# One order of q for scores and relative term, and the rows' scalings moved from VectorE to ScalarE

## The chip, the core and the metric

The kernel runs on one core of a Trainium2 chip. The core has TensorE (PE in the profile, its weight loads PEld), VectorE (DVE), ScalarE (ACT), GpSimd (POOL) and SyncE (SP), which here does nothing but issue DMA transfers and wait. Each engine works through its own instructions in the order in which the program has them. Engines wait for each other by semaphores. The metric is the device time of the whole kernel in microseconds.

## The reference

Four batches of 1024 tokens with 128 features go through attention with 16 heads of 8 features, causal, with a relative term, and then through a feed-forward net. Cut to what matters here:

```python
q, k, v = split_heads(x @ Wq + bq), split_heads(x @ Wk + bk), split_heads(x @ Wv + bv)   # x is normalised per row
scores = jnp.einsum('bhid,bhjd->bhij', q, k)
rel = jnp.einsum('bhid,pd->bhip', q, rel_key)                # P = 256 rows of rel_key
rel_idx = jnp.clip(j - i + p - 1, 0, p - 1)
bias = jnp.take_along_axis(rel, rel_idx, axis=3)
logits = jnp.where(causal, (scores + bias) * scale, -inf)
attn = softmax(logits); out = attn @ v; y = out @ Wo + bo
x = x + layernorm(y)
x = x + layernorm(ffn(layernorm(x)))                         # 128 -> 512 -> 512 -> 512 -> 128
```

## The kernel before, in words

There are three stages, all of them written out in program order by hand. The change is in stage one and in what stage two reads.

Stage one (`sync_one`, `gpsimd_one`, `vector_one`, `scalar_one`, `tensor_one`) goes over the batches b = 0 to 3, and each round of it works on two batches at once. For batch b+1 VectorE makes the statistics of the rows (L482 to L489), ScalarE the root (`std`, L630), VectorE the reciprocal and the offset (`rstd`, `nmr`) and the eight scalings of 128x128 (`xh`, L501). TensorE transposes `xh` into the PSUM tile `p_tr` (L731), ScalarE copies that to `xT` (L637), and TensorE projects it to q and k (L741) and to v (L749). For batch b ScalarE takes q and k out of PSUM (`qf` L664, `kf` L666); VectorE reduces k to extremes (`k_ext`), makes `k_sel` and `own`; TensorE computes from them a bound on the scores, again in `p_tr` (`bound`, L759 to L761). The bound's maximum goes to `gap_max` (L508), the bound itself as two bf16 parts to `m_parts` (ScalarE L699, VectorE L513). The next transposes write into the same `p_tr`, so they wait for both (`transposes` waits `s_mneg`, `s_gap` and `s_mr`).

q and k are written as three bf16 parts each (`q_parts`, `k_parts`: a part 0 by ScalarE, the remainder by VectorE, part 1 by ScalarE, part 2 by VectorE) and stored to DRAM (`q_dram`, `k_dram`) part by part by SP, since stage two needs each of them on other partitions. Stage two also needs q in a second order. Its scores (L1089) take blocks of 128 neighbouring rows i, its relative term (L1023) takes for one r of 128 the rows r, 128 + r, 256 + r and so on, eight a head. The kernel before stores q twice: `q_dram` in the order of the rows, and `qr_dram` with the eight rows of one r side by side. The second comes from `turn_query` (L650), which has ScalarE copy each of the three parts into `q_turned`. The remainder of batch b+1's parts can only start when the stores of batch b's parts have landed (L681, L682).

SP's order in batch 1 matters: it stores batch 0's bound, waits until all stores of batch 0 have landed, issues the loads of stage two's first unit (`q_rows` L413, `k_sb` L334, `q_sb` L323), and then the stores of batch 1.

Stage one ends with the first fill of stage two's table `even_b`: TensorE makes eight chunks (`relative`), six copied by ScalarE (L1036) and two by VectorE (L619, L620). ScalarE then does the three `turn_query` of batch 3 and, at L716, waits for `s_low`, which VectorE raises after its two chunks (`low_k`, L532). Stage two takes units of 8 heads: scores and relative chunks on TensorE, additions on VectorE, exponentials on ScalarE, products with v on TensorE. Stage three is the feed-forward net.

## Time and profile before

| | us |
|---|---|
| median of 3 runs | 739.33 |
| lowest and highest | 736.46, 739.54 |
| the profiled execution | 737.71 |
| its span, first to last instruction | 735.6 |
| TensorE busy | 645.0 |
| ScalarE busy | 572.5 |
| VectorE busy | 538.9 |
| DMA moved | 52.82 MB |

2.1 us of the profiled execution lie outside its span. The median of the runs is 1.6 us above the profiled execution. Stage one takes the first 103 to 107 us, stage two runs until about 480 to 490 us, stage three to the end. A busy share is an average over the three and says little on any one of them; what follows is read by stage.

### The profile page before, as it was taken

To read this page: it belongs to the slowest core of one execution; us is meant where nothing else is said; L and a number is where in the kernel's file an instruction comes from. 1 tells how busy PE (TensorE), PEld (TensorE's weight loads), DVE (VectorE), ACT (ScalarE), POOL (GpSimd) and SP (SyncE) were. 2 spreads that over 40 slices of the span, in tenths; PEclk is the share of its full clock that TensorE was granted. 3 is DMA by queue.
4 is the path that set the end of the run, shared out by engine and by line. 5 is a ranking of instruction groups with operands and counts; after the bars stand their busy time and mean duration, and the time that the engine had idled before them with its cause. 6 is when DMAs were issued, how large, how long until landed. Compare 5 with 4: busy or idle time off the path is not lost.

```text
span 735.6 us, 18944 instructions
## 1 busy us (share of the span) xinstructions
PE 645.0 (88%) x8066; PEld 467.9 (64%) x8066; DVE 538.9 (73%) x923; ACT 572.5 (78%) x660; POOL 246.6 (34%) x175
## 2 busy tenths in 40 slices
PE   4877669999999999999999999978799898998993
PEld 2333336676766766867667667655588687786682
DVE  5885787787687877786877777765677568588546
ACT  2794977988989889889898898786577868677573
POOL 2100270360640912705408128010271441731801
PEclk9988767999999999999999999997999999999997
DMA  7487423152241231521412314040300000000001
GB/s 229 113 228 219 134 84 90 38 129 66 51 111 40 71 96 35 130 69 43 106 52 68 100 34 123 27 158 1 101 1 1 0 1 1 1 29 0 6 24 59
DMA packets 39175, 52.82 MB, mean 72 GB/s; under 512 B 5656, under 2 KB 29640, under 8 KB 36680
## 3 DMA queue, kind: packets, MB, share of 16 engines
q1 hardware_dynamic: 39088, 51.58, 25.6%
q8 instruction: 65, 1.06, 0.6%
q14 instruction: 22, 0.18, 0.1%
HBM read 39.00 MB, written 11.81 MB: 69 GB/s over the span
## 4 chain that ended last, share of the span: by engine, by line
PE 53%; DVE 13%; ACT 12%; issue 5%; POOL 2%; DVEq 0%; ACTq 0%; POOLq 0%
PE p_o L1114 16%; PE p_s L1089 13%; PE p_z L1788 8%; PE p_z L1791 8%; DVE probs L1215 6%; ACT probs L1332 6%; PE p_s L1023 5%; POOL hid_lo L1709 1%; DVE res L1969 1%; ACT hid_hi L1892 1%; ACT o_acc L1341 1%; ACT even_b L1036 1%; ACT odd_b L1036 1%; PE p_o L1126 1%; DVE hid_lo L1993 1%
## 5 line engine op out<-in xcount | busy, mean ns | idle before, releaser
L1089 PE MATMUL p_s<-q_sb,k_sb 96*128 96x128 bf16 (+1 forms) x1600 | 172.2, 250 | 9.2 <-ACT probs L1332 3.5
L1332 ACT ACTIVATE probs<-p_s 128x1024 f32<-128x1024 f32 x160 | 156.6, 1017 | 18.5 <-DVE p_s L1224 10.8
L1114 PE MATMUL p_o<-probs,v_sb 128*32 128x128 f32 (+1 forms) x3200 | 159.7, 331 | 7.5 <-ACT o_acc L1341 4.7
L992 POOL TENSOR_SCALAR_AFFINE_SELECT even_b<-even_b 128x2048 f32<-128x2048 f32 x31 | 75.9, 2449 | 259.6 <-ACT even_b L1036 259.6
L1332 ACT ACTIVATE probs<-probs 128x1024 f32<-128x1024 f32 x128 | 133.5, 1055 | 36.1 <-DVE probs L1215 35.8
L1089 PEld LDWEIGHTS p_s<-q_sb,k_sb 96*128 96x128 bf16 x1600 | 113.9, 100 | 68.5 <-issue 30.3
L1215 DVE TENSOR_TENSOR probs<-p_s,even_b 128x1024 f32<-128x1024 f32 x96 | 114.9, 1218 | 16.8 <-PE p_s L1089 16.8
L1114 PEld LDWEIGHTS p_o<-probs,v_sb 128*32 128x32 f32 x3200 | 84.6, 111 | 40.9 <-issue 13.9
L1788 PE MATMUL p_z<-hid_hi,h_hi 128*128 128x512 f32 x256 | 102.1, 399 | 1.7 <-POOL hid_lo L1709 1.7
L1023 PE MATMUL p_s<-q_rows,rel_w 72*128 72x64 bf16 x2048 | 83.8, 196 | 19.6 <-DVE probs L1215 8.7
L1791 PE MATMUL p_z<-hid_lo,h_hi 128*128 128x512 f32 x256 | 100.9, 394 | 0.0
L1023 PEld LDWEIGHTS p_s<-q_rows,rel_w 72*128 72x128 bf16 x2048 | 75.4, 100 | 30.9 <-DVE probs L1215 11.0
L1993 DVE TENSOR_TENSOR hid_lo<-act_f,hid_hi 128x512 fp32r<-128x512 f32 x64 | 55.6, 881 | 41.5 <-ACT hid_hi L1892 41.4
L996 POOL TENSOR_SCALAR_AFFINE_SELECT even_b<-even_b 128x2048 f32<-128x2048 f32 x31 | 73.8, 2380 | 7.0 <-POOL even_b L992 7.0
L1891 ACT ACTIVATE act_f<-p_z,sh_c 128x512 f32<-128x512 f32 x64 | 44.3, 692 | 28.6 <-PE p_z L1791 28.5
L1236 DVE COPY even_b<-p_s 128x1024 f32<-128x1024 f32 x35 | 42.7, 1220 | 21.3 <-PE p_s L1023 21.0
L1788 PEld LDWEIGHTS p_z<-hid_hi,h_hi 128*128 128x128 f32 x256 | 48.2, 188 | 13.5 <-POOL hid_lo L1709 2.6
L1791 PEld LDWEIGHTS p_z<-hid_lo,h_hi 128*128 128x128 f32 x256 | 48.3, 189 | 10.7
L1236 DVE COPY odd_b<-p_s 128x896 f32<-128x896 f32 x32 | 34.7, 1086 | 23.6 <-PE p_s L1023 22.4
L1215 DVE TENSOR_TENSOR probs<-p_s,odd_b 128x1024 f32<-128x1024 f32 x32 | 39.1, 1222 | 15.0 <-PE p_s L1089 15.0
L1892 ACT ACTIVATE hid_hi<-p_z,sh_c 128x512 fp32r<-128x512 f32 x64 | 44.1, 689 | 0.0
L1709 POOL TENSOR_TENSOR hid_lo<-act_f,hid_hi 128x512 fp32r<-128x512 f32 x32 | 42.4, 1326 | 2.6
(182 smaller groups left out, 846.2 us busy)
## 6 DMA issues: line engine op xcount, KB each, us to landing
k_sb<-k_dram SPq DMA_DIRECT2D x48, 192.0 KB
q_sb<-q_dram SPq DMA_DIRECT2D x16, 576.0 KB
q_rows<-qr_dram SPq DMA_DIRECT2D x42, 192.0 KB
q_dram<-q_parts SPq DMA_DIRECT2D x12, 256.0 KB, 3.0
k_dram<-k_parts SPq DMA_DIRECT2D x12, 256.0 KB, 3.2
qr_dram<-q_turned SPq DMA_DIRECT2D x12, 256.0 KB, 3.4
x_all<-in_L_attn_x_dram SPq DMA_DIRECT2D x4, 512.0 KB, 4.4
every<-in_L_ffn_h_w_dram SPq DMA_DIRECT2D x2, 1024.0 KB, 8.3
```

Of the source, the lines that this page charges most:

```text
L992: nc.gpsimd.affine_select(out=far, in_=near, compare_op=ALU.is_ge, fill=0.0, base=-1 - r, pattern=[[0, QB], [-1, MCH * RCH]], channel_mult ...
L996: nc.gpsimd.affine_select(out=near, in_=near, compare_op=ALU.is_ge, fill=MASKED, base=r, pattern=[[0, QB], [1, MCH * RCH]], channel_multip ...
L1023: last = nc.tensor.matmul(slot[:, x * QB:(x + 1) * QB], rel_w[0:ROWS, w0:w0 + BLK], q[:, r, :, :], start=True, stop=True)
L1089: last = nc.tensor.matmul(slot[:, c:c + n * BLK], k_sb[hg][:, h * S + j * BLK:h * S + (j + 1) * BLK], ap(q_sb[hg], at, [[HG * S, KROWS], [ ...
L1114: last = nc.tensor.matmul(p_o[32 * h:32 * h + 32, at:at + blocks * BLK], v_sb[hg][:, j, h * 32:(h + 1) * 32], probs[n % PBUFS][:, h, col * ...
L1215: last = nc.vector.tensor_tensor(probs[m % PBUFS][:, hp * 2:hp * 2 + 2, :], columns(slot, 0, run), term, ALU.add)
L1236: nc.vector.tensor_copy(to, got).then_inc(t_cd, 1)
L1332: nc.scalar.activation(to, got, ACT.Exp, scale=SCALE).then_inc(t_exp, 1)
L1788: nc.tensor.matmul(to[:, :], whi[w][:, j, cols], hi[j], start=(j == 0), stop=False)
L1791: last = nc.tensor.matmul(to[:, :], whi[w][:, j, cols], lo[j], start=False, stop=(j == len(hi) - 1))
L1892: nc.scalar.activation(hid_hi[k][l % 2][:, o, :], bank(tile)[:, :], ACT.Gelu, scale=sc).then_inc(f_ghi, 1)
L1993: nc.vector.tensor_tensor(hid_lo[k][l % 2][:, o, :], act_f[k][:, o, :], hid_hi[k][l % 2][:, o, :].bitcast(F32), ALU.subtract).then_inc(f_l ...
```

## The change

q is stored in one order only. The 1024 rows of a head are 8 blocks i of 128, and a row in its block is r = 4·s + l. The order before was (i, s, l) in `q_dram` and (s, l, i) in `qr_dram`; now there is (s, i, l) alone (`mixed`), with LO = 4 values of l side by side. The permutation is made by the operations that were there already, in their access patterns: ScalarE's part 0, VectorE's remainder of q, and both parts of the bound. `turn_query`, `q_turned`, `qr_dram` and their waits are gone. The score matmul reads q in runs of four, the relative matmul reads every fourth element. The sign of the bound is no longer turned; the row of k that meets it is -1 in place of 1.

The scalings `xh` of batches 1 to 3 are made by ScalarE (`scaled`), the statistics of batch b+2 stand at the end of VectorE's round b, and ScalarE's check of the weights' low bits (`low_bits`) stands after the parts. `largest_scores`, a branch for inputs with a wide bound that is not taken here, is fitted to the new order.

```diff
-        for copy in range(PARTS):
-            sp.dma_start(to, ap(qr_dram, u * (UH * S) + half * width,
+            sp.dma_start(to, ap(q_dram, u * (UH * S) + half * width,
...
+    def natural(tile):
+        return tile.rearrange("p (i r l) -> p r i l", i=NB, l=LO)
+    def mixed(tile):
+        return tile.rearrange("p (r i l) -> p r i l", i=NB, l=LO)
...
         def batch(b, first, last):
             if b == 1:
-                for done in (s_qst, s_kst, s_rst):
+                for done in (s_qst, s_kst):
                     sp.wait_ge(done, 16 * PARTS)
-                sp.dma_start(q_rows[:, :], ap(qr_dram, 0, [[DROW, PARTS * HD], [0, PARTS], [1, UH * S]])).then_inc(t_qr[0], 16)
+                sp.dma_start(q_rows[:, :], ap(q_dram, 0, [[DROW, PARTS * HD], [0, PARTS], [1, UH * S]])).then_inc(t_qr[0], 16)
...
-                if not last:
-                    turned(b, part)
...
         def layernorm(b, first):
             dve.wait_ge(s_std, b + 1)
+            if not first:
+                dve.wait_ge(s_xh, b)
             nc.vector.reciprocal(rstd[:, :], std[:, :]).then_inc(s_ln, 1)
...
+            if not first:
+                return
             dve.wait_ge(s_ln, b * LNS + 5)
-            if not first:
-                dve.wait_ge(s_tr, b * 2)
             for t in range(NB):
                 last = nc.vector.tensor_scalar(xh[:, t, :], tile(t), rstd[:, t:t + 1], nmr[:, t:t + 1],
                                                ALU.mult, ALU.add)
...
         def shift_rest(b):
-            nc.vector.scalar_tensor_tensor(out=m_parts[:, 1, :], in0=p_tr[0:H, :], scalar=-1.0, in1=m_parts[:, 0, :],
-                                           op0=ALU.mult, op1=ALU.subtract).then_inc(s_mr, 1)
+            nc.vector.tensor_tensor(mixed(m_parts[:, 1, :]), natural(p_tr[0:H, :]), mixed(m_parts[:, 0, :]),
+                                    ALU.subtract).then_inc(s_mr, 1)
...
         def batch(b, first, last_batch):
-            if not last_batch:
-                layernorm(b + 1, False, None if first else lambda: gap(b - 1))
-            else:
+            if not first:
                 gap(b - 1)
-            if not first:
                 shift_rest(b - 1)
...
-            nc.vector.tensor_tensor(q_rest[:, :], qf[:, :], q_parts[:, 0, :], ALU.subtract).then_inc(s_rest, 1)
+            nc.vector.tensor_tensor(mixed(q_rest[:, :]), natural(qf[:, :]), mixed(q_parts[:, 0, :]), ALU.subtract).then_inc(s_rest, 1)
...
+            if b + 2 < B:
+                layernorm(b + 2, False)
...
+        def scaled(b):
+            act.wait_ge(s_xin, b * 16 + 16)
+            act.wait_ge(s_ln, b * LNS + 5)
+            act.wait_ge(s_tr, b * 2)
+            for t in range(NB):
+                last = nc.scalar.activation(xh[:, t, :], x_all[:, b * S + t * E:b * S + (t + 1) * E], ACT.Identity,
+                                            scale=rstd[:, t:t + 1], bias=nmr[:, t:t + 1])
+            last.then_inc(s_xh, 1)
...
-        def turn_query(b, part):
-            nc.scalar.activation(turned_view(q_turned, part), untouched_view(q_parts, part),
-                                 ACT.Identity).then_inc(s_turned, 1)
...
-            nc.scalar.activation(q_parts[:, 0, :], qf[:, :], ACT.Identity).then_inc(s_hi, 1)
+            nc.scalar.activation(mixed(q_parts[:, 0, :]), natural(qf[:, :]), ACT.Identity).then_inc(s_hi, 1)
...
-                nc.scalar.activation(m_parts[:, 0, j * 512:(j + 1) * 512], p_tr[0:H, j * 512:(j + 1) * 512],
-                                     ACT.Identity, scale=-1.0).then_inc(s_mneg, 1)
-            if not last_batch:
-                turn_query(b, 2)
+                nc.scalar.activation(mixed_half(m_parts[:, 0, :], j),
+                                     p_tr[0:H, j * 512:(j + 1) * 512].rearrange("p (i r l) -> p i r l", i=NB // 2, l=LO),
+                                     ACT.Identity).then_inc(s_mneg, 1)
+            if b + 2 < B:
+                scaled(b + 2)
...
-                turn_query(b, 0)
-                turn_query(b, 1)
-                turn_query(b, 2)
...
-        q = q_rows[:, :].rearrange("k (h r i) -> k r h i", h=UH, i=NB)
+        q = q_rows[:, :].rearrange("k (h r i l) -> k r l h i", h=UH, i=NB, l=LO)
-            last = nc.tensor.matmul(slot[:, x * QB:(x + 1) * QB], rel_w[0:ROWS, w0:w0 + BLK], q[:, r, :, :],
+            last = nc.tensor.matmul(slot[:, x * QB:(x + 1) * QB], rel_w[0:ROWS, w0:w0 + BLK], q[:, r // LO, r % LO],
...
-                    at = h * S + i * BLK
+                    at = h * S + i * LO
-                                            ap(q_sb[hg], at, [[HG * S, KROWS], [2 * BLK, n], [1, BLK]]),
+                                            ap(q_sb[hg], at, [[HG * S, KROWS], [2 * LO, n], [NB * LO, BLK // LO], [1, LO]]),
```

Line numbers in the rows of after are those of the changed file, some ten to fifteen lower. ScalarE's queue before, from the bound of batch 1 (`m_parts`) through batch 2:

```order
L699 ACTIVATE m_parts<-p_tr 16x512 x2
L654 ACTIVATE q_turned<-q_parts 128x1024
L630 ACTIVATE std<-var_e 128x8
L664 ACTIVATE qf<-p_q,bq_c 128x1024
L666 ACTIVATE kf<-p_k,kb_c 128x1024
L637 ACTIVATE xT<-p_tr 128x512 x2
L674 ACTIVATE q_pos<-qf 128x1024
L683 ACTIVATE q_parts<-qf 128x1024
L685 ACTIVATE k_parts<-kf 128x1024
L654 ACTIVATE q_turned<-q_parts 128x1024
L689 ACTIVATE q_parts<-q_rest 128x1024
```

And the same stretch after:

```order
L689 ACTIVATE m_parts<-p_tr 16x4x32x4
L622 ACTIVATE std<-var_e 128x8
L689 ACTIVATE m_parts<-p_tr 16x4x32x4
L637 ACTIVATE xh<-x_all,nmr,rstd 128x128 x8
L656 ACTIVATE qf<-p_q,bq_c 128x1024
L658 ACTIVATE kf<-p_k,kb_c 128x1024
L629 ACTIVATE xT<-p_tr 128x512 x2
L665 ACTIVATE q_pos<-qf 128x1024
L673 ACTIVATE q_parts<-qf 128x1024
L675 ACTIVATE k_parts<-kf 128x1024
L677 ACTIVATE q_parts<-q_rest 128x1024
```

The eight scalings stand where the third `q_turned` of the batch stood; the other two leave no replacement. On VectorE the stretch from the parts of k in batch 0 to the extremes of k in batch 1 reads, before:

```order
L532 TENSOR_TENSOR k_parts<-k_rest,k_parts 128x1024
L482 BN_STATS stats<-x_all 128x6 x8
L486 BN_AGGR mv<-stats 128x2 x8
L489 TENSOR_SCALAR var_e<-mv 128x8
L508 TENSOR_REDUCE gap_max<-p_tr 16x1
L493 RECIPROCAL rstd<-std 128x8
L495 SCALAR_TENSOR_TENSOR nmr<-mv,rstd 128x8
L501 TENSOR_SCALAR xh<-x_all,rstd,nmr 128x128 x8
L513 SCALAR_TENSOR_TENSOR m_parts<-p_tr,m_parts 16x1024
L543 TENSOR_REDUCE k_ext<-kf 128x1
```

and after:

```order
L524 TENSOR_TENSOR k_parts<-k_rest,k_parts 128x1024
L474 BN_STATS stats<-x_all 128x6 x8
L478 BN_AGGR mv<-stats 128x2 x8
L481 TENSOR_SCALAR var_e<-mv 128x8
L485 RECIPROCAL rstd<-std 128x8
L487 SCALAR_TENSOR_TENSOR nmr<-mv,rstd 128x8
L500 TENSOR_REDUCE gap_max<-p_tr 16x1
L505 TENSOR_TENSOR m_parts<-p_tr,m_parts 16x1024
L532 TENSOR_REDUCE k_ext<-kf 128x1
```

The eight `xh` are gone, and the reciprocal stands ahead of `gap_max`. SP's queue after, from the stores of batch 0 to the loads of the first unit (before, a store `qr_dram<-q_turned` stood behind each pair, nine stores a batch in place of six):

```order
L397 DMA q_dram<-q_parts 16x8x1024
L397 DMA k_dram<-k_parts 16x8x1024
L397 DMA q_dram<-q_parts 16x8x1024
L397 DMA k_dram<-k_parts 16x8x1024
L397 DMA q_dram<-q_parts 16x8x1024
L397 DMA k_dram<-k_parts 16x8x1024
L394 DMA m_dram<-m_parts 16x2x1024
L410 DMA q_rows<-q_dram 72x1x8192
```

Nothing else moved on SP there: the loads still wait for the stores of batch 0.

## Rows read from the trace of the kernel before

**Rows 1.** The page: the span.
```profile
span 735.6 us, 18944 instructions
```

**Rows 2.** Busy time in 130 to 480 us (PE, PEld, DVE, ACT, POOL, clock, DMA).
```profile
130.00:480.00 350.00, 330.03 (x6127) 243.43 (x6124) 272.53 (x277) 304.02 (x318) 137.29 (x71) 0.99 0.28 73
```

**Rows 3.** Groups by line and shape, ScalarE, 0 to 110 us (busy, mean ns, idle before).
```profile
L654 ACT ACTIVATE q_turned<-q_parts 128x1024 bf16<-128x1024 bf16 x12 | 23.5, 1978 | 0.0
...
L637 ACT ACTIVATE xT<-p_tr 128x512 f32<-128x512 f32 x8 | 4.7, 596 | 8.9 <-PE p_tr L731 8.9
...
L685 ACT ACTIVATE k_parts<-kf 128x1024 bf16<-128x1024 f32 x4 | 4.2, 1047 | 0.0
...
L630 ACT ACTIVATE std<-var_e 128x8 f32<-128x8 f32 x4 | 0.8, 197 | 5.7 <-DVE var_e L489 5.7
```

**Rows 4.** Timeline, batch 1 and turn to 2 (start, duration, engine, [idle before <-releaser]).
```profile
45.16 0.60 ACT L637 ACTIVATE xT<-p_tr 128x512 f32<-128x512 f32 x1 [0.20 <-PE p_tr L731]
...
57.00 0.59 ACT L699 ACTIVATE m_parts<-p_tr 16x512 bf16<-16x512 f32 x1 [1.93 <-PE p_tr L761]
...
57.50 1.94 ACT L654 ACTIVATE q_turned<-q_parts 128x1024 bf16<-128x1024 bf16 x1
...
59.44 1.09 ACT L664 ACTIVATE qf<-p_q,bq_c 128x1024 f32<-128x1024 f32 x1
...
60.01 2.13 DVE L501 TENSOR_SCALAR xh<-x_all,rstd,nmr 128x128 f32<-128x128 f32 x8
...
62.17 1.21 DVE L513 SCALAR_TENSOR_TENSOR m_parts<-p_tr,m_parts 16x1024 bf16<-16x1024 f32 x1
...
63.53 1.66 PE L731 MATMUL p_tr<-ident,xh 128*128 128x128 f32 x8 [4.58 <-DVE m_parts L513]
64.44 0.60 ACT L637 ACTIVATE xT<-p_tr 128x512 f32<-128x512 f32 x1 [2.91 <-PE p_tr L731]
```

**Rows 5.** Timeline, ScalarE and VectorE, batch 2 and the turn to batch 3.
```profile
72.02 1.06 ACT L683 ACTIVATE q_parts<-qf 128x1024 bf16<-128x1024 f32 x1 [5.25 <-DMA k_dram<-k_parts]
...
73.11 1.23 DVE L566 TENSOR_TENSOR q_rest<-qf,q_parts 128x1024 f32<-128x1024 f32 x1 [5.44 <-ACT q_parts L683]
...
80.81 1.21 DVE L513 SCALAR_TENSOR_TENSOR m_parts<-p_tr,m_parts 16x1024 bf16<-16x1024 f32 x1
...
84.51 1.22 DVE L543 TENSOR_REDUCE k_ext<-kf 128x1 f32<-128x1024 f32 x1 [2.49 <-ACT kf L666]
```

**Rows 6.** Timeline, SP's queue: first and last store of batch 0, loads, batch 1.
```profile
34.56 0.63 SPq L396 DMA_DIRECT2D q_dram<-q_parts  x1
...
40.42 0.74 SPq L396 DMA_DIRECT2D qr_dram<-q_turned  x1
...
44.19 0.84 SPq L413 DMA_DIRECT2D q_rows<-qr_dram  x1
...
56.24 2.62 SPq L396 DMA_DIRECT2D k_dram<-k_parts  x1
```

**Rows 7.** DMA issues from 34.3, 38.2 and 56.2 us (last: us to landing).
```profile
q_dram<-q_parts SPq DMA_DIRECT2D x1, 256.0 KB, 3.0
...
qr_dram<-q_turned SPq DMA_DIRECT2D x2, 256.0 KB, 3.8
...
k_dram<-k_parts SPq DMA_DIRECT2D x1, 256.0 KB, 15.7
```

**Rows 8.** Timeline, VectorE and ScalarE, end of stage one.
```profile
97.15 1.22 DVE L508 TENSOR_REDUCE gap_max<-p_tr 16x1 f32<-16x1024 f32 x1 [1.71 <-PE p_tr L761]
...
101.08 5.80 ACT L654 ACTIVATE q_turned<-q_parts 128x1024 bf16<-128x1024 bf16 x3
...
106.19 1.22 DVE L532 TENSOR_TENSOR k_parts<-k_rest,k_parts 128x1024 bf16<-128x1024 f32 x1
...
107.45 1.94 ACT L1332 ACTIVATE probs<-p_s 128x1024 f32<-128x1024 f32 x2 [0.56 <-DVE k_parts L532]
```

**Rows 9.** The chain that ended last, in stage two (start, duration, what).
```profile
120.04 0.47 PE p_s L1023 x16
```

More of the change, by code:

```diff
@@ L32 @@
 PARTS = 3
+LO = 4
 ROWS = PARTS * PARTS * HD
@@ L253, in build @@
     m_parts = sb("m_parts", [H, MPARTS, S], BF16, one)
-    q_turned = sb("q_turned", [128, PARTS, S], BF16, one)
     pone = ExitStack()
@@ L1471, in head @@
             sp.wait_ge(e_part, g * EPARTS + EPARTS)
-            sp.dma_start(ap(m_dram, g * S, [[BLK, NB], [DROW, MPARTS], [1, BLK]]), parts[:, :, :]).then_inc(e_out, 16)
+            for part in range(MPARTS):
+                sp.dma_start(ap(m_dram, part * DROW + g * S, [[LO, NB], [NB * LO, BLK // LO], [1, LO]]),
+                             parts[:, part, :].rearrange("p (r l) -> p r l", l=LO)).then_inc(e_out, 16)
         with sp.If(taken(sp)):
```

62 lines of the change are left out of this document (23 added, 39 removed).

## The prediction

> **What bounds the kernel now.** I read the stretches first. From 130 to 480 us TensorE is busy 330 of 350 us at a granted clock of 0.99, so stage two is TensorE's, and a change can shorten it only on TensorE [rows 2]. Nothing of the change takes an instruction off TensorE. What can get shorter is stage one, and the chain that ended last is to be followed there by the timeline, queue by queue.
>
> The turn from batch 1 to batch 2 shows how stage one hangs together. The second half of the bound is copied at 57.00 (it waited 1.93 us for TensorE), the third `q_turned` runs from 57.50 for 1.94 us, then `qf` starts at 59.44 and `kf` follows, ending at about 61.5. Meanwhile VectorE scales the rows from 60.01 to 62.14 and only then makes the bound's remainder (`m_parts`, 62.17, 1.21 us). The transposes wait 4.58 us for it and start at 63.53; ScalarE, idle for 2.91 us, copies `xT` from 64.44 [rows 4]. So ScalarE and VectorE hold each other up.
>
> The next place is batch 2. ScalarE cannot write part 0 of q until the stores of batch 1 have landed: it idles 5.25 us until 72.02 on the last `k_dram` store, and VectorE idles 5.44 us behind it [rows 5]. That store was issued at 56.24 and took 15.7 us to land, behind the loads of stage two's first unit, which were issued from 44.19 [rows 6, 7]. From 72.02 VectorE works practically without a gap to the bound's remainder at 80.81, ends it at 82.02, and then waits 2.49 us for ScalarE's `kf`: the extremes of k of batch 3 start at 84.51 [rows 5]. They head the chain of VectorE's work that leads to `own`, to batch 3's bound and with it to the end of stage one.
>
> The last place is that end. ScalarE runs three `q_turned` from 101.08 for 5.80 us, yet the first exponentials, at 107.45, are released by VectorE's `k_parts`, which runs from 106.19 [rows 8].
>
> **The change part by part.** *The twelve `q_turned`.* Each is 1.978 us [rows 3], 23.5 us of ScalarE in all. Nine of them stand in batches 0 to 2. The third of each batch stands ahead of the next `qf`; there the eight scalings take its place. An activation of 8 columns is 0.197 us, one of 512 is 0.596 us [rows 3]; by straight line one of 128 columns is 0.30 us alone, and as two long ones overlap by about 0.1 us (two exponentials take 1.94 us together, [rows 8], where one copy alone is 1.05 us, [rows 3]) a row of eight should take 0.2 us each, 1.6 to 1.9 us. The bounds are 8 x 0.197 = 1.6 and 8 x 0.596 = 4.8 us. I take 1.9, nearest to the line between the rows. So the slot ahead of `qf` stays as it is: 0 us. The last three, 5.8 us, save nothing either, because at 107.45 ScalarE waits for `low_k` (L716), and VectorE's queue there is untouched: 0 us, with 0 to -0.6 as bounds, the 0.56 us of idle time being all that ScalarE's side ever had to do with it [rows 8]. The other `q_turned` of batches 0 to 2 stood beside TensorE's projections and bound and gave ScalarE slack that it now has more of.
>
> *The scalings off VectorE, the remainder of the bound ahead.* 2.13 us go from between `gap_max` and the bound's remainder [rows 4]. After the change `gap_max` (57.0 to 58.2) is followed by the remainder to 59.4, the transposes are done before `kf` ends at 61.5, and `xT` follows `kf` at once: 61.5 in place of 64.44, so 2.9 us a turn. This is gained at two turns, since at the first one (batch 0 to 1) the scalings stay ahead of the transposes on either engine. But the second turn's gain only counts as far as the DMA lets batch 2 go, and so it does not enter the sum; it sets its early bound.
>
> *Six stores a batch in place of nine.* Batch 0's nine stores are issued from 34.56 on; the last, issued at 40.42, lands 3.8 us later at 44.2, and the loads go out at 44.19 [rows 6, 7]. The first landed 3.0 us after its issue [rows 7], at 37.6, so nine took 0.83 us each. Six are through at 37.6 + 5 x 0.83 = 41.7. The loads go out at 41.7 if the bound's remainder of batch 0 has been stored by then, for which SP waits first; without the scalings ahead of it VectorE makes it by about 39.9. That is 2.5 us earlier. Behind the loads the last `k_dram` store had seven stores before it and now has five: 2 x 0.83 = 1.65 us. So it lands at 56.24 + 15.7 - 2.5 - 1.65 = 67.8 in place of 71.94, and ScalarE's part 0 of batch 2 starts at 67.85 in place of 72.02: -4.2 us. Bounds: the loads start no earlier and only the missing stores count, -1.65 us; or the stores land before they are needed.
>
> *The turn from batch 2 to 3.* VectorE started `q_rest` at 73.11 and ended at 82.02, 8.9 us [rows 5], with a gap of 0.3 us for a part that ScalarE made late behind `q_turned`. From 68.95 it ends at 77.6. ScalarE, with no `q_turned` between, copies part 0 of q and k, waits for VectorE, copies parts 1 until about 72.4, copies the bound until 73.4, and ends `kf` at 75.5. VectorE is the later one, so the 2.49 us of idle time are gone and the extremes of batch 3 start at 77.6 in place of 84.51: -6.9 us. The early bound is TensorE's: between `xT` of a batch (45.16) and the copy of its predecessor's bound (57.00) pass 11.8 us from start to start [rows 4]; with the second half of `xT` of batch 3 at about 59.6 the bound's copy starts at 71.4, `qf` at 72, `kf` of batch 3 ends at 74.1, -10.4 us. The late bound, from -1.65 in place of -4.2, is -4.3 us; if nothing at all lands earlier, 71.9 + 9.8 = 81.7, -2.8 us.
>
> *The permutation in ScalarE's and VectorE's own operations.* Part 0 of q, the remainder and the bound now read or write in runs of four elements. The only permuted copy in the trace is `q_turned`, one bf16 element at a time at a stride of 256 bytes, at 1.978 us against 1.047 us for an ordered one [rows 3]. Runs of four f32 lie nearer to the ordered row: 0 us. Were part 0 of q and both bound copies as slow as `q_turned`, 1 to 2 us a batch would come back in three batches, in ScalarE's slack for the most part.
>
> *TensorE's reads.* The relative matmul reads 64 columns, eight bf16 side by side in the row before and now every fourth element; the score matmul reads runs of four with gaps. Sixteen relative matmuls take 0.47 us of the chain, 29 ns each [rows 9]. The new patterns are in no row. Below, nothing can be gained. Above, each read might suffer as ScalarE's did, 1.978 / 1.047 = 1.89 times: 2048 x 29 x 0.89 = 53 us for the relative matmuls alone. I take 0, since the slow row has one element to a place and the new reads have two or four side by side within 16 bytes.
> The Trainium skill ("SBUF — State Buffer", section "Door 1: The DMA port swizzle") has a rule that bears on this: SBUF is read in lines of 16 bytes, and at least two hits in a row on a line are needed for the full rate. `q_turned` has one hit, and the trace agrees with 1.978 us against 1.047. The relative matmul now has two, just enough by the rule, which makes rival A the case in which the rule is too kind to TensorE; no row here shows two hits on TensorE.
>
> **The sum.** 737.7 (span 735.6 and 2.1 outside it, [rows 1]) - 6.9 = 730.8 us. The median of the runs lay 1.6 above the profiled execution; a median is forecast, so I say 731.
>
> **The rivals.** *A, TensorE reads slower.* Place: L1023 and L1089 in stage two, where TensorE has only 20 of 350 us idle [rows 2]. For it: TensorE takes an element from each partition every 0.45 ns (64 columns in 29 ns), over twice as fast as ScalarE (1024 in 1.047 us, [rows 3]), so two neighbours within 16 bytes need not be enough for it. Against it: the slow row has one element to a place, the new pattern two. It ends slower than before from 6.9 / 2048 = 3.4 ns a relative matmul, 12% of 29 ns. At the full factor, relative matmuls alone, 731 + 53 = 784, at a third of it 749.
> *B, the stall stays.* The stores are held by the loads, which are as many bytes as before, and the missing stores save nothing that is waited for; the extremes start at 81.7, -2.8 us: 735. For it: the store before took 15.7 us behind them [rows 7]. Against it: both stores and loads start earlier by SP's own order.
> *C, dear scalings.* Eight at 0.596 us are 4.8, 2.9 more than the slot, in two turns, and 2.6 more in the first. `kf` of batch 3 then ends at about 79.7: -4.8 us, 733. For it: scale and bias come from SBUF per row. Against: the 0.197 us of a small activation with the same engine.
> *D, more gained.* The stores land before batch 2 asks: -10.4 us, 727; in batch 3 TensorE idles less before its bound.
>
> **How the numbers follow.** Forecast with C and D, -4 to -10.4 us: 0.77 (C 0.05, D 0.10). B or a small part of A that eats most of the gain, within 0.5% (3.7 us, about what a measurement of this kernel can tell): 0.10. A, slower: 0.13, of which 0.12 above 743. So faster 0.77, same 0.10, slower 0.13. The likeliest case's own range is 727 to 735, widened by 1.6 at either side for the runs; the 8 in 10 range leaves out A and ends where B does, 725 to 737.
>
> **What would show it.** ScalarE's `q_parts` of batch 2 starting near 68, `xT` of batch 3 right behind `kf`, eight `xh` activations near 0.2 us apart, `k_ext` of batch 3 near 77.6, the first `probs` near 100.5 still released by VectorE's `k_parts`, sixteen L1023 matmuls (a lower line number now) still 0.47 us in stage two and an unchanged length from the first `probs` to the end. It is wrong if relative matmuls last over 32 ns in a row, if `k_dram` still lands at 71, or if the first exponentials gain over a microsecond on VectorE's `k_parts`.

## The result, and the profile after

The changed kernel takes 778.7 us (median of 4 runs, 774.2 to 783.4), the kernel before, run beside it, 738.1 (4 runs). The ratio is 1.055, 95% interval 1.051 to 1.059. The forecast was 731 (725 to 737), faster; it came out slower. The profiled execution took 777.35 us. The first three views of it are the page's span, the stretch 130 to 480 us (columns as in [rows 2]), and TensorE's relative term and its largest group of scores, by line and shape over the whole span; the last line is one step of the chain that ended last and answers to [rows 9].

```profile
span 775.6 us, 18917 instructions
```
```profile
130.00:480.00 350.00, 338.58 (x5486) 260.43 (x5485) 243.88 (x246) 277.41 (x286) 123.27 (x63) 0.99 0.25 65
```
```profile
L1010 PE MATMUL p_s<-q_rows,rel_w 72*128 72x64 bf16 x2048 | 139.4, 235 | 13.1 <-DVE probs L1202 5.2 <-DVE even_b L1223 3.5 <-ACT probs L1319 2.1
L1076 PE MATMUL p_s<-q_sb,k_sb 96*128 96x256 bf16 x704 | 113.1, 278 | 1.9 <-ACT probs L1319 1.2 <-issue 0.3 <-DVE even_b L612 0.3
```
```profile
124.50 0.94 PE p_s L1010 x16
```

L1010 is the old L1023, L1076 the old L1089. Against [rows 2], TensorE is busier (338.6 of 350 us) and gets less done: 5486 matmuls in place of 6127, at the same granted clock of 0.99. Sixteen relative matmuls take 0.94 us in the chain, in place of 0.47: 59 ns each, not 29. Before, the same group had these totals, and the score matmuls of 256 columns were as long as they are now (the kernel before, same view):

```profile
L1023 PE MATMUL p_s<-q_rows,rel_w 72*128 72x64 bf16 x2048 | 83.8, 196 | 19.6 <-DVE probs L1215 8.7 <-ACT kf L666 5.5 <-ACT probs L1332 3.5
L1089 PE MATMUL p_s<-q_sb,k_sb 96*128 96x256 bf16 x704 | 112.8, 279 | 5.6 <-DVE probs L1215 3.0 <-ACT probs L1332 1.3 <-issue 1.2
```

So reading every fourth element costs, reading runs of four doesn't. The busy time of the relative matmuls rose by 55.6 us. In the stretch 130 to 480 us TensorE's idle time fell from 20 to 11.4 us, so a part of the longer reads filled time in which it had waited before.

Stage one gained next to nothing. ScalarE and VectorE in the turn to batch 2, in batches 2 and 3 and at the end, and GpSimd beside them (timelines; the rows answer to [rows 4, 5, 8]):

```profile
56.75 3.18 ACT L637 ACTIVATE xh<-x_all,nmr,rstd 128x128 f32<-128x128 f32 x8
59.84 1.09 ACT L656 ACTIVATE qf<-p_q,bq_c 128x1024 f32<-128x1024 f32 x1
...
61.83 1.06 ACT L629 ACTIVATE xT<-p_tr 128x512 f32<-128x512 f32 x2
...
69.71 1.06 ACT L673 ACTIVATE q_parts<-qf 128x1024 bf16<-128x1024 f32 x1 [5.88 <-DMA k_dram<-k_parts]
...
107.18 1.94 ACT L1319 ACTIVATE probs<-p_s 128x1024 f32<-128x1024 f32 x2 [6.50 <-DVE k_parts L524]
```
```profile
79.25 1.20 DVE L532 TENSOR_REDUCE k_ext<-kf 128x1 f32<-128x1024 f32 x1
...
81.61 1.50 DVE L537 TENSOR_TENSOR k_ext<-k_ext,g_ext 128x2 f32<-128x2 f32 x1
...
83.33 4.72 DVE L545 TENSOR_SCALAR k_sel<-hmask,k_ext 128x64 f32<-128x64 f32 x2
87.96 1.27 DVE L549 SCALAR_TENSOR_TENSOR own<-kf,g_ext,qf 128x1024 f32<-128x1024 f32 x1
...
90.29 2.22 DVE L555 TENSOR_TENSOR q_rest<-qf,q_parts 128x1024 f32<-128x1024 f32 x1
...
96.19 1.22 DVE L500 TENSOR_REDUCE gap_max<-p_tr 16x1 f32<-16x1024 f32 x1 [2.55 <-PE p_tr L749]
...
105.92 1.23 DVE L524 TENSOR_TENSOR k_parts<-k_rest,k_parts 128x1024 bf16<-128x1024 f32 x1
```
```profile
80.75 2.36 POOL L979 TENSOR_SCALAR_AFFINE_SELECT even_b<-even_b 128x2048 f32<-128x2048 f32 x1 [46.13 <-ACT even_b L1023]
83.34 2.36 POOL L983 TENSOR_SCALAR_AFFINE_SELECT even_b<-even_b 128x2048 f32<-128x2048 f32 x1 [0.23 <-POOL even_b L979]
85.65 2.36 POOL L979 TENSOR_SCALAR_AFFINE_SELECT even_b<-even_b 128x2048 f32<-128x2048 f32 x1
88.23 3.22 POOL L983 TENSOR_SCALAR_AFFINE_SELECT even_b<-even_b 128x2048 f32<-128x2048 f32 x1 [0.23 <-POOL even_b L979]
```

The operations of GpSimd are its selects, which make the masks in the table `even_b`. `k_ext` of batch 3 starts at 79.25, 5.3 us earlier than in [rows 5]. But then two small operations of VectorE last as long as GpSimd's selects: the first ends at 83.11, when the select that began at 80.75 ends (80.75 + 2.36), and `k_sel`, 128x64 elements twice, ends at 88.05 with the third select (88.01). In the kernel before, the first select came 7.1 us later, when `k_sel` was done:

```profile
87.27 0.42 DVE L556 TENSOR_SCALAR k_sel<-hmask,k_ext 128x64 f32<-128x64 f32 x2
87.61 1.28 DVE L560 SCALAR_TENSOR_TENSOR own<-kf,g_ext,qf 128x1024 f32<-128x1024 f32 x1
```
```profile
87.85 3.25 POOL L992 TENSOR_SCALAR_AFFINE_SELECT even_b<-even_b 128x2048 f32<-128x2048 f32 x1 [53.39 <-ACT even_b L1036]
```

So `own` starts at 87.96, not earlier than the 87.61 of before, `gap_max` is 1.0 us and the first exponentials are 0.3 us earlier than in [rows 8]. From the first exponentials to the end it is 668.4 us (775.6 - 107.18), before 628.2 (735.6 - 107.45): the loss lies in the part that reads the new order.

Two questions follow: which read costs, and by what rule; and what takes back the gain of stage one.

### The profile page after: what moved, and what is told of

It reads as the page before. It is cut to its first block, busy times and chain, and to the rows that moved or that the text cites. A ratio compares the mean times of both kernels' runs of the same rounds, so it can differ in the third digit from the quotient of the medians.

```text
span 775.6 us, 18917 instructions
## 1 busy us (share of the span) xinstructions
PE 692.6 (89%) x8066; PEld 516.7 (67%) x8066; DVE 536.1 (69%) x899; ACT 565.0 (73%) x672; POOL 245.3 (32%) x175
## 3 DMA queue, kind: packets, MB, share of 16 engines
q8 instruction: 65, 1.06, 0.6%
## 4 chain that ended last, share of the span: by engine, by line
PE 60%; DVE 16%; ACT 6%; issue 3%; POOL 2%; DVEq 0%; POOLq 0%; ACTq 0%
PE p_o L1101 16%; PE p_s L1076 13%; PE p_s L1010 12%; PE p_z L1781 7%; PE p_z L1784 7%; DVE probs L1202 7%; ACT probs L1319 2%; POOL hid_lo L1702 1%; DVE p_s L1207 1%; DVE res L1962 1%; DVE even_b L1223 1%; ACT hid_hi L1885 1%; PE p_o L1113 1%; DVE hid_lo L1986 1%; PE p_pre L1722 1%
## 5 line engine op out<-in xcount | busy, mean ns | idle before, releaser
L1319 ACT ACTIVATE probs<-p_s 128x1024 f32<-128x1024 f32 x160 | 158.9, 1020 | 43.4 <-PE p_s L1076 18.0
L1076 PE MATMUL p_s<-q_sb,k_sb 96*128 96x128 bf16 (+1 forms) x1600 | 169.2, 246 | 3.7 <-ACT probs L1319 1.5
L979 POOL TENSOR_SCALAR_AFFINE_SELECT even_b<-even_b 128x2048 f32<-128x2048 f32 x31 | 73.8, 2381 | 282.3 <-ACT even_b L1023 275.4
L1076 PEld LDWEIGHTS p_s<-q_sb,k_sb 96*128 96x128 bf16 x1600 | 114.2, 99 | 60.6 <-issue 35.0
L1010 PE MATMUL p_s<-q_rows,rel_w 72*128 72x64 bf16 x2048 | 139.4, 235 | 13.1 <-DVE probs L1202 5.2
L1010 PEld LDWEIGHTS p_s<-q_rows,rel_w 72*128 72x128 bf16 x2048 | 125.1, 113 | 23.6 <-DVE probs L1202 7.3
L1101 PEld LDWEIGHTS p_o<-probs,v_sb 128*32 128x32 f32 x3200 | 83.8, 111 | 42.9 <-issue 11.0
L1986 DVE TENSOR_TENSOR hid_lo<-act_f,hid_hi 128x512 fp32r<-128x512 f32 x64 | 54.5, 862 | 42.9 <-ACT hid_hi L1885 42.7
L983 POOL TENSOR_SCALAR_AFFINE_SELECT even_b<-even_b 128x2048 f32<-128x2048 f32 x31 | 73.9, 2385 | 7.0 <-POOL even_b L979 6.7
L1223 DVE COPY even_b<-p_s 128x1024 f32<-128x1024 f32 x35 | 42.8, 1222 | 36.7 <-PE p_s L1010 36.7
L1023 ACT ACTIVATE odd_b<-p_s 128x896 f32<-128x896 f32 x32 | 29.2, 913 | 20.6 <-PE p_s L1010 19.8
```

The lines of the kernel that those rows point to most:

```text
L979: nc.gpsimd.affine_select(out=far, in_=near, compare_op=ALU.is_ge, fill=0.0, base=-1 - r, pattern=[[0, QB], [-1, MCH * RCH]], channel_mult ...
L983: nc.gpsimd.affine_select(out=near, in_=near, compare_op=ALU.is_ge, fill=MASKED, base=r, pattern=[[0, QB], [1, MCH * RCH]], channel_multip ...
L1010: last = nc.tensor.matmul(slot[:, x * QB:(x + 1) * QB], rel_w[0:ROWS, w0:w0 + BLK], q[:, r // LO, r % LO], start=True, stop=True)
L1076: last = nc.tensor.matmul(slot[:, c:c + n * BLK], k_sb[hg][:, h * S + j * BLK:h * S + (j + 1) * BLK], ap(q_sb[hg], at, [[HG * S, KROWS], [ ...
L1101: last = nc.tensor.matmul(p_o[32 * h:32 * h + 32, at:at + blocks * BLK], v_sb[hg][:, j, h * 32:(h + 1) * 32], probs[n % PBUFS][:, h, col * ...
L1223: nc.vector.tensor_copy(to, got).then_inc(t_cd, 1)
```

## The experiments

Each ran on the chip beside the kernel before, whose medians lay between 737.2 and 739.2 us; ratios are against it. The table has the start of the first exponentials (probs) and the span, both of one profiled execution each. That execution can lie off the median: for before_read it is the slowest of 4 (784.3), for two_masks the fastest of 13 (735.2). The starts vary as well: before_read changes nothing before the table's fill in batch 3, yet ScalarE waits 7.02 us for batch 1's last store in place of 5.25. A difference of a microsecond or two between two starts is thus not evidence by itself; the medians and the lengths of operations are.

| kernel | median us | ratio, 95% interval | probs | span |
|---|---|---|---|---|
| before | 738.1 | | 107.45 | 735.6 |
| changed | 778.7 | 1.055 (1.051, 1.059) | 107.18 | 775.6 |
| side: changed, neighbours read | 735.9 | 0.998 (0.996, 1.000) | 106.60 | 733.8 |
| before_read: before, every fourth read | 781.0 | 1.057 (1.054, 1.060) | 109.72 | 782.2 |
| lo2: changed, LO = 2 | 841.2 | 1.140 (1.134, 1.145) | 106.13 | 840.1 |
| lo1: LO = 1 | 1263.0 | 1.712 (1.706, 1.719) | 112.79 | 1260.9 |
| lo8: LO = 8 | 911.9 | 1.233 (1.226, 1.241) | 105.94 | 916.5 |
| side_dve: side, scalings by VectorE | 736.4 | 0.998 (0.996, 1.000) | 107.11 | 732.4 |
| side_masks: side, masks late | 733.7 | 0.994 (0.992, 0.996) | 104.00 | 731.7 |
| two_orders: before, order of stage one | 738.6 | 1.000 (0.998, 1.002) | 108.75 | 736.8 |
| two_masks: two_orders, masks late | 740.5 | 1.003 (1.001, 1.004) | 108.33 | 733.5 |
| before_masks: before, masks late | 740.9 | 1.003 (1.001, 1.005) | 109.82 | 738.4 |
| cheap_turn_masks: changed, cheap ordered copy, masks late | 742.2 | 1.005 (1.003, 1.006) | 111.16 | 740.0 |
| best: that, low_k early | 735.5 | 0.996 (0.994, 0.997) | 106.45 | 734.3 |
| late_lowk_sp: cheap_turn_masks, store moved | 735.3 | 0.995 (0.994, 0.997) | 105.45 | 733.6 |
| best_sp: best, store moved | 735.9 | 0.995 (0.993, 0.997) | 103.84 | 734.2 |

### Which read costs

The first kernel is the changed one with one read put back, so that the relative term takes q values of other rows:

```diff
-        q = q_rows[:, :].rearrange("k (h r i l) -> k r l h i", h=UH, i=NB, l=LO)
+        q = q_rows[:, :].rearrange("k (h r i) -> k r h i", h=UH, i=NB)
...
-            last = nc.tensor.matmul(..., rel_w[0:ROWS, w0:w0 + BLK], q[:, r // LO, r % LO],
+            last = nc.tensor.matmul(..., rel_w[0:ROWS, w0:w0 + BLK], q[:, r, :, :],
```

> The changed kernel with one difference: the relative matmuls (L1010) read eight neighbouring elements of q, as they did before the change, from the rows that are stored in the new order. Their values are so those of other rows of q; everything else is as in the changed kernel. Theory (the read of every fourth element halves TensorE's rate): sixteen relative matmuls fall from 0.93 back to 0.47 us, time about 778.7 - 40 = 738. Rival (the stored order or the scores' runs of four cost the time, through the loads or the score matmuls): it stays within 5 us of 778.

The mirror of it is the kernel before with the other read, again with values of other rows:

```diff
-        q = q_rows[:, :].rearrange("k (h r i) -> k r h i", h=UH, i=NB)
+        q = q_rows[:, :].rearrange("k (h r i l) -> k r l h i", h=UH, i=NB, l=4)
...
-            last = nc.tensor.matmul(..., rel_w[0:ROWS, w0:w0 + BLK], q[:, r, :, :],
+            last = nc.tensor.matmul(..., rel_w[0:ROWS, w0:w0 + BLK], q[:, r // 4, r % 4],
```

> The kernel before, changed in one place: the 2048 relative matmuls read every fourth of 32 neighbouring elements of q_rows (two in each 16 bytes) where they read eight neighbours; they thus take q values that belong to other rows, and nothing else moves. Theory 'lines' (TensorE reads at full rate only with four wanted bf16 in each 16 bytes; two of them cost 58 ns in place of 29 per 64 columns): sixteen relative matmuls take 0.93 us in the chain, 0.195 us more mean by line, and the time is 738 + 41 = 779 us, within 3. Theory 'whole change' (the loss needs the new storage, the scalings or the new order of stage one beside the read): 738 us, and sixteen stay at 0.47 us.

They mirror each other in time, too: 735.9 and 781.0. The relative matmuls by line, of side and of before_read:

```profile
L1010 PE MATMUL p_s<-q_rows,rel_w 72*128 72x64 bf16 x2048 | 82.8, 195 | 15.8 <-DVE probs L1202 8.7 <-ACT probs L1319 3.5 <-DVE even_b L612 1.2
```
```profile
L1023 PE MATMUL p_s<-q_rows,rel_w 72*128 72x64 bf16 x2048 | 139.5, 235 | 18.3 <-ACT kf L666 6.0 <-DVE probs L1215 5.2 <-DVE even_b L1236 3.5
```

This one access pattern is the whole loss, with either form of stage one: 42.8 us from side to changed, 42.9 from before to before_read. What else the change did is worth 1.3 us (side against its own kernel before, 737.2), an interval that just reaches no change. before_read lies 2 us above the 779 of its expectation, within the 3 us given there.

### By what rule

LO is the number of neighbours that the storage keeps together. The scores then read runs of LO, the relative term every LO-th element. The theory of lines says that the 16 bytes of SBUF that hold an element (a line) are what is paid for, and counts the wanted bf16 in each line touched: the scores have LO of them, the relative term 8 / LO. Three kernels change one number (`LO = 4` to 2, 1, 8).

> LO = 2: the relative matmul reads every second element (4 bytes apart), the scores read pairs with gaps. Three theories. (8 bytes) TensorE needs two wanted elements in each 8 bytes: both patterns have them, relative matmuls 29 ns, scores unchanged, about 738. (neighbours) only directly neighbouring elements go at full rate: relative matmuls stay at 58 ns, scores unchanged, about 778. (lines) it is wanted elements per 16 bytes, and four are needed: relative matmuls back to 29 ns, but the scores' pairs now double, 294912 columns at 0.42 ns more, about 738 + 120 = 858.

> LO = 1: the relative matmul reads eight neighbours, the scores read single elements 16 bytes apart. All theories: relative matmuls at 29 ns, scores at half rate; four score matmuls of 256 columns 1.0 in place of 0.54 us, up to 120 us more than 738, so about 850. If the scores have slack, less. If a 16 byte pitch costs more than an 8 byte pitch, over 900.

> LO = 8: the relative matmul reads elements 16 bytes apart, one to each 16 bytes; the scores read runs of eight. (8 bytes) one wanted element in 8 bytes costs the same as at LO = 4: 58 ns, about 778. (lines) one to each 16 bytes instead of two costs double again, 116 ns: about 778 + 100 = 880.

Steps of the chain that ended last, of lo2 (four score matmuls of 256 columns, and the relative term), of the kernel before (the same four), and of lo8 (the relative term), all at a granted clock of 1.00:

```profile
118.52 1.02 PE p_s L1076 x4
119.54 0.47 PE p_s L1010 x16
```
```profile
119.50 0.54 PE p_s L1089 x4
```
```profile
121.90 1.81 PE p_s L1010 x16
```

| wanted bf16 in 16 bytes | ns for 64 columns | from |
|---|---|---|
| 8 | 29 | before, relative, 0.47 / 16 |
| 4 | 29 | lo2, relative, 0.47 / 16 |
| 2 | 59 | changed, relative, 0.94 / 16 |
| 2 | 64 | lo2, scores, 1.02 / 4 for 256 columns, a quarter of it |
| 1 | 113 | lo8, relative, 1.81 / 16 |

The numbers fit one price, 1.8 to 2.0 ns for each 16 bytes touched (16, 32 and 64 of them in 64 columns), and a floor of 0.45 ns a column under it. It doesn't matter which matmul reads: at two in 16 bytes the scores nearly double as well (1.02 for 0.54 us), and lo2 is slow by them alone, its relative term back at 29 ns. The theory of neighbours fails on this relative term, the theory of 8 bytes on lo2's scores and on lo8.

The times themselves agree less well. lo2 takes 841 us where the lines gave 858. lo8 takes 912 where they gave 880, with a granted clock of 0.88 in 130 to 480 us in place of 0.99, so it holds a clock loss too. lo1 takes 1263 where 850 was expected, or over 900.

The price of 16 bytes does not follow the clock. From 110 to 115 us the granted clock is 0.50, the level of 1.2 GHz, in before, changed and lo8 alike. Sixteen relative matmuls there, of before, changed and lo8:

```profile
113.89 0.92 PE p_s L1023 x16
```
```profile
113.84 0.92 PE p_s L1010 x16
```
```profile
114.25 1.78 PE p_s L1010 x16
```

lo8 pays the same as at 1.00 (1.81). The changed kernel pays nothing at all: a column lasts so long at this clock that two elements in 16 bytes keep up. Of the counts tried, four are needed at 2.4 GHz, and two are enough at 1.2.

No LO serves both reads: the relative term wants at most 2, the scores at least 4.

The Trainium skill ("SBUF — State Buffer", section "Door 1: The DMA port swizzle") asks for two hits a line. For TensorE at 2.4 GHz the measurement decides against it: two cost double, four are enough (three were not tried). At 0.50 of the clock, and for ScalarE, it holds. Part 0 of q by ScalarE reads f32, four to 16 bytes; it takes two of them at LO = 2 and one at LO = 1 (groups by line of lo2 and lo1, 0 to 110 us):

```profile
L673 ACT ACTIVATE q_parts<-qf 128x1024 bf16<-128x1024 f32 x4 | 4.4, 1093 | 5.5 <-DMA k_dram<-k_parts 5.5
```
```profile
L673 ACT ACTIVATE q_parts<-qf 128x1024 bf16<-128x1024 f32 x4 | 7.8, 1951 | 2.4 <-DMA k_dram<-k_parts 2.4
```

One f32 to 16 bytes costs 1951 / 1024 = 1.9 ns, and so does one bf16 in the `q_turned` of [rows 3] (1978 / 1024): the same price as TensorE's. VectorE's `q_rest` of batch 2 takes 1.95 us in lo1 and 1.23 in lo2, again 1.9 ns. What differs is the time that an engine has for an element, 1.0 ns on ScalarE and 0.45 on TensorE, and with it how many elements must share the price. That the price has one common cause is not shown.

lo1 shows one thing more, its stretch 130 to 480 us:

```profile
130.00:480.00 350.00, 350.00 (x2608) 171.77 (x2601) 119.52 (x117) 134.46 (x134) 58.84 (x30) 0.50 0.12 31
```

TensorE counts as busy for the whole stretch, yet the granted clock is 0.50, its level of 1.2 GHz. So busy time doesn't show that a matmul waits for its operand. The scores, read at one element to 16 bytes, are 217 of the 350 us. lo1's 1263 us hold a clock loss beside the read: sixteen relative matmuls, whose read is ordered there, last 0.85 us in place of 0.47. Why the clock stays down wasn't tested apart.

### What takes back the gain of stage one

The next two kernels build on side, so that stage two is as before. First, what the change's scalings are worth:

```diff
-            if not first:
-                return
+            if not first:
+                dve.wait_ge(s_tr, b * 2)
...
-                scaled(1)
...
-            if b + 2 < B:
-                scaled(b + 2)
```

> Run side with the scalings of batches 1 to 3 back on VectorE, ahead of the bound's maximum. Eight scalings took 3.18 us on ScalarE, 2.14 on VectorE. If the DMA sets batch 2 and GpSimd's selects the end, it is 735 to 738, no difference to side. If ScalarE's dear scalings delay the loads and batch 2 by their 1.3 us a turn, it is 1 to 2 us faster than side.

736.4 against 735.9, overlapping intervals: whether ScalarE or VectorE makes the scalings is worth nothing that can be measured. Then, GpSimd's selects are held until VectorE has made the remainders of batch 3, the last batch; where an expectation speaks of batch 1 here, batch 3 is meant:

```diff
+        pool.wait_ge(s_rest, B * 2)
```

> The kernel of run side (relative matmuls read eight neighbours, so values of other rows of q) and one wait more: GpSimd starts its first masks of even_b only when VectorE has made both remainders of batch 3. Theory (GpSimd's selects hold VectorE's f32 work on SBUF up): k_sel of batch 3 falls from 4.72 us for two to 0.42, own starts near 83 in place of 87.4, the first exponentials at about 102 in place of 106.6, time 735.9 - 4.5 = 731.4. Rival (VectorE is late for another reason, or the masks then come late): k_sel stays at 4 us, or the first addition waits for GpSimd, 736 or more.

Its VectorE, batch 3 and the end, GpSimd's last select ahead of the exponentials, and ScalarE:

```profile
79.65 1.20 DVE L533 TENSOR_REDUCE k_ext<-kf 128x1 f32<-128x1024 f32 x1
...
82.40 0.42 DVE L546 TENSOR_SCALAR k_sel<-hmask,k_ext 128x64 f32<-128x64 f32 x2
82.73 1.28 DVE L550 SCALAR_TENSOR_TENSOR own<-kf,g_ext,qf 128x1024 f32<-128x1024 f32 x1
...
90.86 1.22 DVE L501 TENSOR_REDUCE gap_max<-p_tr 16x1 f32<-16x1024 f32 x1 [3.45 <-PE p_tr L750]
...
100.69 3.28 DVE L525 TENSOR_TENSOR k_parts<-k_rest,k_parts 128x1024 bf16<-128x1024 f32 x1
```
```profile
100.55 2.36 POOL L984 TENSOR_SCALAR_AFFINE_SELECT even_b<-even_b 128x2048 f32<-128x2048 f32 x1 [0.23 <-POOL even_b L980]
```
```profile
104.00 1.94 ACT L1320 ACTIVATE probs<-p_s 128x1024 f32<-128x1024 f32 x2 [9.12 <-DVE k_parts L525]
```

`k_sel` is back at 0.42 us and `gap_max` comes 5.3 us earlier than in the changed kernel. That the selects held VectorE is therefore shown. It is a hold both ways: in the changed kernel the select that begins at 88.23, 0.27 us after `own`, lasts 3.22 us in place of 2.36. Some of the gain is lost again: the last `k_parts` meets a select that began 0.14 us before it, and ends 1.06 us after that (3.28 in place of 1.23 us). The exponentials are 2.6 us earlier than in side, where 4.6 were expected, and the time is 2.2 us shorter (733.7 for 735.9; 3.1 us by the two ratios), where 4.5 were. The Trainium skill ("SBUF — State Buffer", section "Who interferes with whom") says when the two contend: VectorE in a two-port mode, or VectorE with two SBUF inputs against a GpSimd operation that reads SBUF. The later one blocks in full. The trace agrees, with 4.72 us for 0.42 us of work; no run shows in which mode `k_sel` ran.

Then the order of stage one (scalings on ScalarE, statistics at the end of the round, low bits later) in the kernel before, with its twelve `q_turned` and two orders of q kept, alone and with the late masks; and the late masks in the kernel before itself:

> The kernel before with the other half of the change alone: scalings of batches 1 to 3 by ScalarE, statistics at the end of VectorE's round, low bits later. q is still turned by ScalarE and stored twice (the third turn of a batch stands between the two halves of the bound). If this half is what brings stage one forward, the extremes of batch 3 start at 80 to 82 (84.5 before) and GpSimd's selects eat it again: time 736 to 738, no difference to before. If the missing stores were what counts, the extremes stay at 84 and the time at 737 to 739.

> two_orders with GpSimd's first masks behind both remainders of batch 3. Theory of GpSimd's selects: 2 to 4 us under two_orders, 733 to 735, faster than before by 3 to 4 us. Rival (selects do not matter where the extremes start late, as in the kernel before): as two_orders.

> The kernel before, with only GpSimd's wait ahead of the masks (they start after the remainders of batch 1's parts). Theory 'the chain decides': k_ext of batch 3 is late there anyway (84.5), and GpSimd's selects only held k_sel for 0.42 us at 87.27, so nothing is gained: 737 to 739.5 us. Rival 'the masks cost in every order': own comes as much earlier as in the changed kernel with that wait, and the time is 734 to 736 us.

738.6, 740.5 and 740.9 us: none is faster, and the two with late masks are slower by 0.3% (0.1 to 0.5%). Two expectations missed: two_masks was to gain 3 to 4 us, before_masks to end by 739.5. With `q_turned` in ScalarE's queue `k_ext` of batch 3 starts at 84.10 in two_orders, without it at 79.38 in side_dve, where VectorE makes the scalings. The gain of stage one thus came from `q_turned` and its stores leaving, not from the scalings; copies and stores were not taken apart.

The selects hold VectorE in the kernel before, too, only at another operation:

```profile
92.09 3.36 DVE L568 TENSOR_TENSOR k_rest<-kf,k_parts 128x1024 f32<-128x1024 f32 x1
```
```profile
91.33 3.05 POOL L996 TENSOR_SCALAR_AFFINE_SELECT even_b<-even_b 128x2048 f32<-128x2048 f32 x1 [0.23 <-POOL even_b L992]
```

In before_masks `k_rest` is back at 1.22 us, and the last `k_parts` meets a select instead (2.75 us). two_masks is alike: `k_sel` falls from 2.60 to 0.42 us and `k_rest` from 3.36 to 1.22, `gap_max` comes 2.4 us earlier, but the exponentials only 0.4, behind a `k_parts` of 2.47 us. Late masks move the collision, and what they win early can be gone by the end. Why these two kernels end slower is not shown.

### A version that beats both

An ordered copy of q is needed for the relative term. Made from the mixed order it should be cheap, as ScalarE then finds two wanted elements in each 16 bytes. The masks are late in all four kernels from here on. The store of batch 2's copies goes between batch 3's stores:

```diff
+            nc.scalar.activation(q_turned[:, part, :].rearrange("p (r l i) -> p r l i", i=NB, l=LO),
+                                 q_parts[:, part, :].rearrange("p (r i l) -> p r l i", i=NB, l=LO),
+                                 ACT.Identity).then_inc(s_turned, 1)
...
                 sp.wait_ge(made, b * 2 + 2)
+                if b == B - 1:
+                    turned(b - 1, part)
```

> The changed kernel with a second, ordered copy of q kept for the relative term: q_turned is made by ScalarE from the mixed order (it reads two wanted elements in each 16 bytes and writes eight neighbours), is stored behind the stores of q and k, and the relative matmuls read eight neighbours of it; GpSimd starts its masks only after the remainders of batch 1's parts, as in the run before that. If ScalarE pays nothing for two in 16 bytes (as its part 0 did at LO = 2: 1093 ns) each copy is 1.05 to 1.15 us, not 1.98, the relative matmuls are back at 0.47 us for sixteen, and the first exponentials come at 104 to 106 us: 733 to 736 us. If ScalarE pays as TensorE does, each copy is 1.9 us or more and the time is 737 to 740. If the extra stores hold batch 2's parts back by more than 2 us, 736 to 739 with copies at 1.1 us.

The copies are cheap, but the time is 742.2, slower than before by 0.3 to 0.6%. Of this kernel, the group of the copies, and the wait ahead of the last three:

```profile
L673 ACT ACTIVATE q_turned<-q_parts 128x1024 bf16<-128x1024 bf16 x11 | 11.9, 1110 | 11.7 <-DMA qr_dram<-q_turned 11.7
```
```profile
108.14 3.11 ACT L673 ACTIVATE q_turned<-q_parts 128x1024 bf16<-128x1024 bf16 x3 [11.67 <-DMA qr_dram<-q_turned]
```

1110 ns against the 1978 of [rows 3]. The next kernel moves `low_k` of batch 3 up, behind `low_q`:

```diff
+        low_k(B - 1)
...
-        low_k(B - 1)
```

> The kernel just described, with low_k of batch 3 (VectorE's part 2 of k, which releases the first exponentials) moved up right behind low_q, ahead of what VectorE does for the flags and table copies. If GpSimd's select held low_k at the end, as the trace of the run with late masks suggests (3.28 us in place of 1.2), the first exponentials come 1 to 2 us earlier than in the kernel without the move: 731 to 734 us. If only the order is changed and the same work is due before the first exponentials anyway, there is no difference over 0.5 us.

735.5 us, 0.4% faster than the kernel before (interval 0.3 to 0.6%), but the reason of the expectation is not the right one. `low_k` still meets a select, and ScalarE still waits, for less long (best, VectorE and ScalarE):

```profile
97.09 3.36 DVE L541 TENSOR_TENSOR k_parts<-k_rest,k_parts 128x1024 bf16<-128x1024 f32 x1
```
```profile
103.39 3.17 ACT L673 ACTIVATE q_turned<-q_parts 128x1024 bf16<-128x1024 bf16 x3 [6.57 <-DMA qr_dram<-q_turned]
```

SP stores batch 2's third copy only after its wait for `low_k` of batch 3, and the last three `q_turned` wait for that store. The last two kernels take this store ahead of the wait, with `low_k` early and late:

```diff
+                if b == B - 1 and part == 2:
+                    turned(b - 1, part)
                 sp.wait_ge(made, b * 2 + 2)
-                if b == B - 1:
+                if b == B - 1 and part < 2:
                     turned(b - 1, part)
```

> The same move in SP's queue, but with low_k left behind VectorE's copies into the table. In the run without it ScalarE waited 11.67 us on the store until 108.14 and the first exponentials came at 111.16, with low_k done at 105.2. If the store order ate the 6.6 us between the two kernels, this one gains 6 us or more: the exponentials at 104 to 106 and 733 to 736 us. If low_k's place was worth it by itself, it stays at 739 to 742.

> The kernel with the cheap turned copies, late masks and low_k moved up, with one store moved in SP's queue: the third turned part of batch 2 goes out ahead of SP's wait for batch 3's part 2 and no longer behind it. In the run without this move ScalarE waited 6.57 us on a qr_dram store until 103.39 and the first exponentials came at 106.45, although low_k was done at 100.45. Theory 'the store order ate it': that wait is gone, the turned copies of batch 3 run from 97 to 100, the first exponentials come between 100.5 and 103.5, and of those 3 to 6 us 2 to 4 are left at the end, because VectorE's copies into the table still end near 105: 731 to 734 us. Rival 'the table decides': VectorE's four copies, moved behind low_k, set the start of stage two either way, and the time stays at 735 to 736.5 us.

With `low_k` late the move brings 6.9 us (742.2 to 735.3, span 740.0 to 733.6): the store's place in SP's queue was the whole difference to best. With `low_k` early it brings none: the exponentials start 2.6 us earlier, at 103.84, but TensorE's next relative chunk still waits for VectorE's table, as TensorE's timeline of best_sp shows:

```profile
105.87 1.03 PE L1054 MATMUL p_s<-q_rows,rel_w 72*128 72x64 bf16 x16 [1.23 <-DVE even_b L633]
```

In best the same chunk waits 1.23 us as well, until 105.36, and the first products with v start at 113.73 there, at 113.53 here. So the rival was right: the table decides. Three versions end at 735.3 to 735.9 and can't be told apart. Each is faster than the kernel before by 0.4 to 0.5%, clear of the interval but small, and than the changed one by 43 us.

## Why the prediction was wrong

*TensorE's reads: 0 us taken, 43 measured* (side to changed). This is the step that failed: "the slow row has one element to a place and the new reads have two or four side by side within 16 bytes". Two and four are not alike: four cost nothing (278 ns against 279 for the scores), two cost the full factor of two at 2.4 GHz. The prediction set a row of ScalarE beside a read of TensorE, and a rule without an engine's rate. It had in rival A the reason that the runs bear out (an element each 0.45 ns, over twice ScalarE's rate) and its upper price, 784 us, but gave it 0.12. That 784 lies near the measured 779 is in part luck: its base of 731 was 5 us too low, its 53 us for the read 10 too high. By the rows A's price is now 2048 x 29 ns = 59 us, an estimate. TensorE's busy time rose by 52.7 us (639.9 in side, 692.6 in changed), the span by 41.8; the 10.9 between the two were idle time of TensorE that the longer reads filled.

*The scalings.* 1.9 us taken, 3.18 measured, 479 ns for one by the groups and 0.40 from start to start. The line through an 8-column and a 512-column activation was too kind; rival C's place was right, its size between. `qf` comes at 59.84 in place of 59.44, and `xT` follows `kf` at once, as forecast (61.83 for 61.5).

*The stores.* SP issues the loads at 41.94 (forecast 41.7), but ScalarE's part 0 of batch 2 starts at 69.71, not 67.85: -2.3 us in place of -4.2. The term that failed is the one for the missing stores, 1.65 us: the last `k_dram` store is issued at 54.04, 2.2 us earlier, and lands 15.7 us later, as long as before. The late bound, -1.65, is nearer in size, but its reason (the loads no earlier, the missing stores all of it) is the reverse of what happened. `k_ext` of batch 3 comes at 79.25, forecast 77.6, before 84.51: -5.3 of -6.9 us, three quarters. The order of events was right. The early bound of that turn, -10.4 us, doesn't follow from the prediction's own times: it starts from the second half of `xT` at 59.6, where `xT` was forecast to begin at 61.5; from 62.1 it is -7.9.

*What is late next.* After `k_ext` the sum had the chain move on as a block. In the kernel before `k_sel` took 0.42 us at 87.27, ahead of the first select at 87.85. In the changed kernel both come early, `k_sel` by 3.9 us and the first select by 7.1, and now the selects are there first: of 5.3 us 0.3 are left at the exponentials. No semaphore links the two operations, so following waits could not show it. side_masks shows it, and what the change's stage one is worth with the collision moved: 2 to 3 us on top of side, not the 5 that `k_ext` had gained.

*Permutation in the own operations:* 0 us, right. Part 0 of q is 1047 ns with runs of four, as the ordered copy in [rows 3].

*The signs named there.* Relative matmuls over 32 ns in a row (59) showed it wrong. The other two conditions did not come: the last `k_dram` store landed before 69.71, not at 71, and the exponentials follow VectorE's `k_parts` at once (105.92 + 1.23 = 107.15, then 107.18). The exponentials were to start near 100.5, though, and they did not.

## What to carry to other kernels

Before a layout is shared by two readers, count for each the wanted elements in every 16 bytes: TensorE needs four bf16 at its full clock, ScalarE two. A slow ordered copy off the bound engine can be cheaper than a free layout that the bound engine reads badly, and it can often be made cheap by choosing the order that it copies from. A step pulled forward may land beside another engine's SBUF work that no semaphore shows; look at what runs at its new time. A queue issues in order, so a store behind a late wait is itself late, whoever waits for it.
